# Group norm in pairs of token tiles, a residual shift ahead of the gates, a folded scale, and three rounding passes on GpSimd in a two-layer decoder

## The reference

```python
# gated memory, per token and head: h = values weighted by gates / (maxit + 1e-6)
xn = (h - mean(h)) / sqrt(var(h) + 1e-5)          # over the 32 channels of a head
out = xn * gn_w + gn_b
# quantised feed-forward
def act_quant(x):
    scale = 127.0 / clip(max(abs(x), -1), 1e-5)
    return clip(round(x * scale), -128, 127) / scale
h = act_quant(x) @ weight_quant(w1).T             # 256 -> 1024
h = silu(depthwise_conv(h))
y = act_quant(h) @ weight_quant(w2).T             # 1024 -> 256
```

## Time and profile before

| | |
|---|---|
| median of three runs | 827.95 us |
| the profiled execution | 829.15 us |
| its span, first to last instruction | 827.6 us |
| TensorE busy (matmuls) | 739.1 us, 89% |
| VectorE busy | 574.9 us, 69% |
| ScalarE busy | 358.0 us, 43% |
| GpSimd busy | 170.3 us, 21% |
| filler matmuls | 38 |

### The profile page before, as it was taken

One profiled execution on the slowest core, in us unless ns is written; L12 is line 12 of the kernel. 1 busy time (PEld: TensorE's weight loads), 2 busy tenths in 40 slices (PEclk: granted clock), 3 DMA queues, 4 the chain that ended last, 5 costly groups with the idle time before them and its releaser, 6 DMA issues.

```text
span 827.6 us, 14805 instructions
## 1 busy us (share of the span) xinstructions
PE 739.1 (89%) x5876; PEld 495.7 (60%) x5933; DVE 574.9 (69%) x1477; ACT 358.0 (43%) x654; POOL 170.3 (21%) x257
## 2 busy tenths in 40 slices
PE   9999999989999968799969999999999978975494
PEld 5776565766566755567644576867547757554232
DVE  1568554674476778988899964657465777798786
ACT  2675214242255226476238534243344431683253
POOL 8611001210006120004330030201003631014201
PEclk9999999999999978699989999999999998988597
DMA  9501000000010100013100030000000000000001
GB/s 347 226 14 64 0 1 1 2 2 2 27 51 27 28 1 2 0 52 103 27 0 1 2 102 1 2 1 2 1 1 1 2 2 2 0 2 2 0 1 51
DMA packets 12740, 23.77 MB, mean 29 GB/s; under 512 B 768, under 2 KB 7040, under 8 KB 12416
## 3 DMA queue, kind: packets, MB, share of 16 engines
q1 hardware_dynamic: 12672, 22.82, 8.0%
HBM read 20.72 MB, written 2.10 MB: 28 GB/s over the span
## 4 chain that ended last, share of the span: by engine, by line
PE 70%; DVE 19%; issue 5%; ACT 3%; POOL 2%; DVEq 0%; ACTq 0%; POOLq 0%
PE bank L753 13%; PE bank L571 7%; PE bank L563 7%; PE bank L597 4%; PE bank L851 4%; PE bank L763 3%; PE bank L618 3%; PE bank L1103 3%; PE bank L832 2%; PE bank L739 2%; PE bank L798 2%; PE bank L874 2%; DVE stats L1194 1%; PE bank L556 1%; POOL small L2213 1%
## 5 line engine op out<-in xcount | busy, mean ns | idle before, releaser
L2143 POOL TENSOR_TENSOR rstd<-rstd,minus_half 128x2 f32<-128x2 f32 x56 | 42.6, 761 | 501.1 <-DVE rstd L1200 500.9
L753 PE MATMUL bank<-work,f0w 128*128 128x512 f16 x512 | 114.7, 379 | 0.1
L753 PEld LDWEIGHTS bank<-work,f0w 128*128 128x128 f16 x512 | 49.4, 98 | 59.6 <-issue 1.9
L1926 ACT ACTIVATE work<-bank 128x512 f16<-128x512 f32 x64 | 36.7, 598 | 44.9 <-PE bank L753 33.6
L1410 DVE SCALAR_TENSOR_TENSOR work<-bank,work 128x512 f16<-128x512 f32 x64 | 42.2, 684 | 15.8 <-ACT work L1926 15.5
L1964 ACT ACTIVATE work<-bank 128x512 f32<-128x512 f32 x32 | 19.1, 596 | 73.2 <-PE bank L851 73.1
L618 PE MATMUL bank<-work 128*128 128x256 f32 x208 | 49.9, 382 | 0.0
L851 PE MATMUL bank<-work 64*128 64x128 f32 x512 | 39.0, 294 | 5.0 <-issue 3.2
L2213 POOL TENSOR_TENSOR small<-small,minus_half 128x8 f32<-128x8 f32 x16 | 26.9, 1678 | 69.8 <-DVE small L1647 69.8
L618 PEld LDWEIGHTS bank<-work 128*128 128x128 f32 x208 | 37.6, 190 | 5.3 <-issue 0.5
L1275 DVE TENSOR_REDUCE small<-bank 128x1 f32<-128x512 f32 (+3 forms) x32 | 18.7, 585 | 31.0 <-PE bank L599 20.3
(11 more groups left out here) (310 smaller groups left out, 1727.5 us busy)
## 6 DMA issues: line engine op xcount, KB each, us to landing
work<-in_mask SPq DMA_DIRECT2D x4, 1024.0 KB, 10.3
xT<-in_xT SPq DMA_DIRECT2D x4, 512.0 KB, 4.1
ctxT<-in_ctxT SPq DMA_DIRECT2D x4, 512.0 KB, 6.5
perf_w<-in_k SPq DMA_DIRECT2D x3, 512.0 KB, 12.1
perf_w<-in_perf_w SPq DMA_DIRECT2D x1, 1536.0 KB, 6.1
x<-in_x SPq DMA_DIRECT2D x2, 512.0 KB, 12.3
ctx<-in_w SPq DMA_DIRECT2D x2, 512.0 KB, 12.2
work<-in_w SPq DMA_DIRECT2D x1, 1024.0 KB, 13.7
```

Of the source, the lines that this page charges most:

```text
L753: ins = nc.tensor.matmul(u.bank[:, :], f0w1[:, k, m * P:(m + 1) * P], s.h1[part][:, k, :], start=(k == 0 and part == 0), stop=(k == NF - 1 ...
L1926: nc.scalar.activation(dst[0][:, m, :], u.bank[:, :], ACT.Relu).then_inc(s.high_made.sem, 1)
L2143: nc.gpsimd.tensor_tensor(s.rstd[:, two], s.rstd[:, two], minus_half[:, 0:2], ALU.pow).then_inc(s.rstd_made.sem, 1)
```

## The change

- The group norm works on pairs of tiles. `ratio` stays by tile; the two tiles' results lie in one buffer (`s.pair`, over the weighed keys). The four small operations, the product with gn_w, the square, the reduction, the power, the scale and the residual add are issued once for two tiles. The product is written to y and scaled in place. The order is ratio 0, 1, square, variance of pair 0; the same for pair 1; then scale, stats and normalize of pair 0 and of pair 1. GpSimd has both powers ahead of both rstd.
- GpSimd adds gn_b to the residual ahead of weighing the keys.
- ScalarE's copy of the first scale row multiplies by f1_scale; `hidden` becomes a product of two tensors.
- GpSimd issues finish_q for blocks 1, 3 and 5; the semaphore for rounded blocks becomes two, and the wait of the mask's load covers both.
- TURNS is written anew for all five queues, and KEEP too: 74 entries with 140 fillers for 26 with 38. By stream and round: (0, 0) 5 to 31, (1, 0) 5 to 43, (0, 1) 5 to 31, (1, 1) 23 to 35.

```diff
--- before.py
+++ after.py
@@ -35,46 +35,57 @@
 ROUNDS = B // STREAMS
 TURNS = {
...
 KEEP = {
-    "perf.spread.0 0 0": 1, "mlstm.out2 0 0": 1, "quant.turn1 0 0": 1, "quant.hidden0 0 0": 2, "sign.xT0 0 1": 1,
-    "sign.xT1 0 1": 2, "perf.spread.1 0 1": 1, "quant.turn1 0 1": 1, "sign.xT0 1 0": 1, "perf.fq.1 1 0": 1,
-    "perf.state.1 1 0": 1, "mlstm.out0 1 0": 1, "perf.spread.0 1 1": 1, "perf.fk.1 1 1": 1, "perf.ft.1 1 1": 2,
-    "perf.state.1 1 1": 1, "mlstm.cols 1 1": 1, "mlstm.out0 1 1": 1, "mlstm.out1 1 1": 1, "mlstm.before3 1 1": 1,
-    "quant.turn0 1 1": 3, "quant.turn1 1 1": 1, "quant.hidden0 1 1": 1, "quant.taps0 1 0": 1, "quant.topT 1 1": 7,
-    "quant.row2 1 1": 2
...
+    "quant.row1 0 0": 3, "quant.topT 0 0": 2, "self.score0 0 1": 1, "self.turn0 0 1": 1, "self.turn2 0 1": 1,
+    "self.product1 0 1": 1, "cross.q1 0 1": 1, "cross.product2 0 1": 1, "sign.xT0 0 1": 6, "sign.early 0 1": 6,
...
+    "quant.topT 0 1": 6, "self.score2 1 0": 1, "self.turn3 1 0": 3, "cross.xT0 1 0": 1, "cross.xT1 1 0": 1,
+    "cross.turn0 1 0": 4, "perf.v0 1 0": 1, "perf.qk.0 1 0": 1, "perf.state.0 1 0": 4, "perf.fk.1 1 0": 6,
+    "perf.ft.1 1 0": 4, "perf.state.1 1 0": 2, "perf.score1.1 1 0": 1, "perf.score3.1 1 0": 1, "perf.out0 1 0": 3,
...
+    "quant.row1 1 1": 1, "quant.turn1 1 1": 1, "quant.hidden0 1 1": 1, "quant.taps0 1 0": 1, "quant.topT 1 1": 6,
+    "quant.row2 1 1": 3
 }
@@ -263,6 +274,8 @@
...
     f1_scale = sb("f1_scale", [P, 2])
+    by_gpsimd = (1, 3, 5)
+
     class Stream:
...
@@ -321,15 +334,14 @@
...
         s.l_state = w.cut(NT - 1, NC, LHT, LV1)
-        s.tmps = [w.cut(LH, LV1),
-                  s.kw[:, 0:2, :, :].rearrange("p a h d -> p (a h d)")[:, 0:LH * LV1].rearrange("p (h d) -> p h d", d=LV1)]
+        s.pair = s.kw[:, :, :, :].rearrange("p a h d -> p (a h d)")[:, 0:NT * LH * LV1].rearrange(
+            "p (q t h d) -> p q t h d", q=2, t=2, d=LV1)
         s.part2_row = w.cut(2, T, dt=BF16, parts=LH)
...
         s.edge = s.small[:, 224:248].rearrange("p (t h) -> p t h", h=LH)
-        s.l_den = s.small[:, 128:128 + LH]
-        s.y_groups = s.y[:, :, :].rearrange("p t (h d) -> p (t h) d", d=LD)
+        s.l_den = s.small[:, 104:104 + 2 * LH].rearrange("p (t h) -> p t h", t=2)
         s.den2, s.var = s.small[:, 160:160 + NT * LH], s.small[:, 192:192 + NT * LH]
-        s.sq = [s.rest[:, j, 0:LH * LD].rearrange("p (g d) -> p g d", d=LD) for j in range(2)]
+        s.sq = [s.rest[:, j, :].rearrange("p (t h d) -> p t h d", t=2, d=LD) for j in range(2)]
 
...
@@ -365,12 +377,16 @@
...
         s.decayed = signal("scores_decayed", LH)
-        s.squared, s.group_var, s.group_rstd = (signal(name, NT) for name in ("group_squared", "group_variance", "group_rstd"))
+        s.squared, s.group_var, s.group_rstd = (signal(name, 2) for name in ("group_squared", "group_variance", "group_rstd"))
 
...
         s.compared, s.scaled_hidden = signal("size_compared", NF - 1), signal("hidden_scaled", NF - 1)
-        s.magic_added, s.q2_made = signal("magic_added", NF), signal("hidden_rounded", NF)
+        s.magic_added = signal("magic_added", NF)
+        s.rounded_v = signal("hidden_rounded_by_vector", NF - len(by_gpsimd))
+        s.rounded_g = signal("hidden_rounded_by_gpsimd", len(by_gpsimd))
+        s.q2_made = [(s.rounded_g, by_gpsimd.index(j)) if j in by_gpsimd else (s.rounded_v, j - sum(i < j for i in by_gpsimd))
+                     for j in range(NF)]
         return s
...
@@ -1138,7 +1154,7 @@
...
                 for k in range(NF):
-                    pe.wait_ge(*s.q2_made.at(n, k))
+                    pe.wait_ge(*s.q2_made[k][0].at(n, s.q2_made[k][1]))
                     for t, u in enumerate(several):
...
@@ -1596,15 +1612,12 @@
...
                         ALU.mult).then_inc(u.emptied, 1)
-            weighed = [None] * NT
+            weighed = [None] * 2
 
...
                 yield f"mlstm.ratio{t}"
-                u, tmp = s.banks["mlstm", n, "out", t], s.tmps[t % 2]
-                if t >= 2:
-                    dve.wait_ge(*s.squared.at(n, t - 2))
-                    dve.wait_ge(*weighed[t - 2])
-                if t == 1:
+                u, tmp = s.banks["mlstm", n, "out", t], s.pair[:, t // 2, t % 2, :, :]
+                if t == 0:
                     dve.wait_ge(*s.banks["mlstm", n, "state", NT - 1].full)
...
@@ -1621,56 +1634,62 @@
                     dve.wait_ge(*u.full)
                     dve.wait_ge(*s.banks["mlstm", n, "cols"].read)
                     nc.vector.tensor_copy(tmp, here).then_inc(u.emptied, 1)
-                yield f"mlstm.square{t}"
-                dve.wait_ge(*u.read)
-                at = col["e", t]
-                m = vec.mark(nc.vector.scalar_tensor_tensor(out=s.l_den, in0=tmp[:, :, LD], scalar=-1.0, in1=tmp[:, :, LD],
-                                                            op0=ALU.mult, op1=ALU.max))
+
+            def of_groups(p):
+                return s.y[:, 2 * p:2 * p + 2, :].rearrange("p t (h d) -> p t h d", d=LD)
+
+            def square(p):
+                yield f"mlstm.square{p}"
+                for t in (2 * p, 2 * p + 1):
+                    dve.wait_ge(*s.banks["mlstm", n, "out", t].read)
+                at, g, den = col["e", 2 * p], slice(2 * p * LH, (2 * p + 2) * LH), s.pair[:, p, :, :, LD]
+                m = vec.mark(nc.vector.scalar_tensor_tensor(out=s.l_den, in0=den, scalar=-1.0, in1=den, op0=ALU.mult, op1=ALU.max))
                 dve.wait_ge(*m)
-                m = vec.mark(nc.vector.tensor_tensor(s.l_den, s.l_den, s.cols[:, at:at + LH], ALU.max))
+                m = vec.mark(nc.vector.tensor_tensor(s.l_den, s.l_den, s.cols[:, at:at + 2 * LH].rearrange("p (t h) -> p t h", t=2),
+                                                     ALU.max))
                 dve.wait_ge(*m)
 
                 m = vec.mark(nc.vector.tensor_scalar(s.l_den, s.l_den, 1e-6, 1e18, ALU.add, ALU.min))
                 dve.wait_ge(*m)
-                vec.mark(nc.vector.scalar_tensor_tensor(out=s.den2[:, t * LH:(t + 1) * LH], in0=s.l_den, scalar=EPS, in1=s.l_den, op0=ALU.mult, op1=ALU.mult))
-                weighed[t] = vec.mark(nc.vector.tensor_tensor(
-                    s.rest[:, t % 2, C:2 * C].rearrange("p (h d) -> p h d", d=LD), tmp[:, :, 0:LD],
-                    gn_w.rearrange("p (h d) -> p h d", d=LD), ALU.mult))
-
-            def variance(t):
-                yield f"mlstm.var{t}"
-                g = slice(t * LH, (t + 1) * LH)
-                dve.wait_ge(*s.squared.at(n, t))
-                m = vec.mark(nc.vector.tensor_reduce(s.var[:, g], s.sq[t % 2], AX, ALU.add))
+                vec.mark(nc.vector.scalar_tensor_tensor(out=s.den2[:, g].rearrange("p (t h) -> p t h", t=2), in0=s.l_den, scalar=EPS,
+                                                        in1=s.l_den, op0=ALU.mult, op1=ALU.mult))
+                weighed[p] = vec.mark(nc.vector.tensor_tensor(
+                    of_groups(p), s.pair[:, p, :, :, 0:LD],
+                    gn_w.rearrange("p (h d) -> p h d", d=LD).unsqueeze(1).broadcast_to([P, 2, LH, LD]), ALU.mult))
+
+            def variance(p):
+                yield f"mlstm.var{p}"
+                g = slice(2 * p * LH, (2 * p + 2) * LH)
+                dve.wait_ge(*s.squared.at(n, p))
+                m = vec.mark(nc.vector.tensor_reduce(s.var[:, g].rearrange("p (t h) -> p t h", t=2), s.sq[p], AX, ALU.add))
                 dve.wait_ge(*m)
-                dve.wait_ge(*weighed[t])
+                dve.wait_ge(*weighed[p])
                 nc.vector.scalar_tensor_tensor(out=s.var[:, g], in0=s.var[:, g], scalar=1.0 / LD, in1=s.den2[:, g],
                                                op0=ALU.mult, op1=ALU.add).then_inc(s.group_var.sem, 1)
 
             added = [None] * NT
 
-            def scale(t):
-                yield f"mlstm.scale{t}"
-                dve.wait_ge(*s.group_rstd.at(n, t))
-                dve.wait_ge(*weighed[t])
-                g = slice(t * LH, (t + 1) * LH)
-                m = vec.mark(nc.vector.tensor_tensor(s.y_groups[:, g, :], s.rest[:, t % 2, C:2 * C].rearrange("p (g d) -> p g d", d=LD),
-                                                     s.var[:, g].unsqueeze(2).broadcast_to([P, LH, LD]), ALU.mult))
+            def scale(p):
+                yield f"mlstm.scale{p}"
+                dve.wait_ge(*s.group_rstd.at(n, p))
+                g, two = slice(2 * p * LH, (2 * p + 2) * LH), slice(2 * p, 2 * p + 2)
+                m = vec.mark(nc.vector.tensor_tensor(
+                    of_groups(p), of_groups(p),
+                    s.var[:, g].rearrange("p (t h) -> p t h", t=2).unsqueeze(3).broadcast_to([P, 2, LH, LD]), ALU.mult))
                 dve.wait_ge(*m)
-                dve.wait_ge(*s.shifted.at(n, 2 * NT + t))
-                added[t] = vec.mark(nc.vector.tensor_tensor(s.y[:, t, :], s.y[:, t, :], x_of(s, n)[:, t, :], ALU.add))
-
-            for i in range(NT + 2):
-                if i >= 2:
-                    yield from scale(i - 2)
```

(78 more changed lines are left out.)

13 lines of the change are left out of this document (7 added, 6 removed), and 60 rows, old and new, of tables (KEEP, TURNS).

## The result

The changed kernel takes 837.11 us (median of 4 runs, 835.78 to 839.38), the kernel before 827.81 beside it: ratio 1.0117, 95% interval 1.0104 to 1.0131. It is 9 us slower; 813.0 was forecast, and the range, 801 to 833, does not hold it.

A forecast was written before the change was run, and what follows sets the result against it. VectorE or engine round trips bound the layer tails, TensorE the sign feed-forward. Norm 10.5, passes 3 - 1, gn_b 0.5, folded scale 0.5, clock 9, fillers -7: 15.5 us saved, median 813; range 801 to 833, forecast's own 805 to 819.

The forecast's parts named there:

- What bounds the kernel: Limits differ by stage: TensorE in a stream's sign feed-forward, VectorE or engine round trips in its layer's tail, including the norms.
- The sum: All terms over the whole span: 10.5 + (3 - 1) + 0.5 + 0.5 + 9 - 7 = 15.5 us saved.
- The new order itself I take at 0: Rewritten weave of both streams on all five queues: 0 us, with -6 to +8, as no row shows it.
- Norm by pairs: Four group norms: 10.7 us less VectorE work, 10.5 us of span (2, 2.6, 1.5 and, in the last, 4.4).
- the first pair's power hides behind ratio 2, ratio 3 and the second pair's work: In each norm, GpSimd's first power of 16 columns, about 2.9 us, is covered by some 3.9 us of other work.
- Passes on GpSimd: Rounding of blocks 1, 3, 5: 3 us saved on the path, 1 us lost to contention; 0.8 us a pass.
- gn_b and the folded scale: Additions moved ahead of key weighing, and the hidden pass without its scalar: 0.5 us saved by each.
- Fillers +7, clock -9: TensorE: 102 more filler matmuls cost 7 us, a third of 22; the higher clock gives back 9 us.
- Order, 0 with -6 to +8: New weave of both streams' steps on all five queues, taken as worth nothing within those bounds in us.
- The first: Rival: fillers land on TensorE's path ahead of real matmuls, costing 15 to 22 us; 837 us; slower, chance 0.17.
- The third: Rival: pair's round trips (powers, rstd0) eat the norm's gain, other stream doesn't close up; 825 to 829 us; same, 0.09.
- The fourth: Rival: GpSimd's twelve passes hold VectorE for 8 us by contention; 821 us; chance 0.15, shared with half the gain.

## Why the prediction was wrong, point by point

*What bounds the kernel.* Held. The norm and the roundings lie in VectorE's stretches, and the last norm, from its first ratio to the last scaling, went from 25.1 to 784.18 - 765.48 = 18.7 us, below the 21 forecast, in spite of the wait for the passes (15.7, from 761.96 to 777.66, with all rounding on VectorE).

*The sum.* 15.5 us less was forecast, 9.7 more measured. 13.1 of these 25.2 us are the norm, gn_b, the folded scale and the order together (-11.5 forecast, +1.6 measured: 1.0019), 10.8 the passes on GpSimd (-2 forecast, +8.8 measured), 1.3 the fillers with the clock. So two steps failed: "The new order itself I take at 0", and the passes, taken at 0.8 us each and hidden.

*Norm by pairs, -10.5 us.* The work was sized rightly (8.8 us of VectorE measured alone, 10.7 summed), and so was the power. The step "the first pair's power hides behind ratio 2, ratio 3 and the second pair's work" held in the changed kernel: VectorE waits for no power of the norm there, and for the last norm's two roots 0.58 us and next to nothing once the passes are gone, where 1.3 and 0.8 were put. What failed is that this reaches the end. In the new order the norms seem to give their 11 us, and the lags lose as much outside them. In before's order, which has no such cover, the first and third norms were +3.5 (and +2.6 behind it) and +3.8, the second 0 and the last -2.6 in place of -4.4, and the power's wait is shown to be the cause.

*Passes on GpSimd, -3 and +1.* The largest error that experiments isolate: +8.8. The price was taken from a select on bf16, 0.64 us, and bounded by doubling two-input operations; but GpSimd's time goes by the operations in a pass, and no row behind the two bounds has a subtraction and a minimum over fp32. At 2.0 us against some 1.5 for VectorE to make the next block, it does not keep pace, as the working has it. Nor did the working ask where in GpSimd's own queue a pass stands, and at three of four places that is part of the price. Contention was there, but small. Of VectorE's instructions that ran beside a pass, the products L1786 (677 ns in the mean against 680 without the passes) and L1676 and L1681 of the last norm kept their length; its own rounding passes took 467 against 420 ns, the 4-column product L1794 493 against 222 (three of its four beside a pass), and two normalising passes (L1225) 0.73 us each, a usual one being 0.41. Added up that is 2.6 us in place of the 1 us of the sum. The Trainium skill's rule on shared interfaces (GPSIMD Engine Reference, Key points) names instructions in a 2-port mode and those with two SBUF inputs: the trace doesn't agree with it for the two products of the last norm, both of whose inputs lie in SBUF, though such products did get longer beside GpSimd's two-input weighing, and no run shows the mode of the others. The advice of its section Engine selection, elementwise work on VectorE, held.

*gn_b and the folded scale, -0.5 each.* Nothing alone, within the interval; 3.6 us with the pairs. Which of the two helps them was not tried apart.

*Fillers +7, clock -9.* The net, -2, was near the measured one (-0.7, within the intervals of 0), and both halves were about right: in the lags the fillers cost some 8 us and the clock gave back some 7. The clock rose as forecast (0.964 against 0.97). In 300 to 320 us it went from 1.2 GHz for most of the stretch to 2.4 GHz throughout, which is where 5.4 us come from, and the 16 matmuls of L571 took 3.72 us in place of 6.72. The changed kernel itself is 7.9 us behind before at 298 us and 2.9 at 317. By the Trainium skill (TensorE: Matmul & The Clock Gate, Part 1), activity releases the lower level; the trace agrees, and the fillers that did it cost as much elsewhere.

*Order, 0 with -6 to +8.* Put on top of the pairs as they stand in before's order it is -1.5. Against what the norm was to give in it, it is the 13 us above, more than its upper bound. The cause stays open; the places are 247 to 273 and 705 to 750 us.

*The rivals.* The first gave 837 and was right by accident: in the new order the fillers' cost is balanced by the clock, and only in before's order does their net come to 11 us. The third, savings that do not reach the end, describes the changed kernel without its passes (828.8, in its 825 to 829), though not by the round trips that it names, which that order hides. The fourth gave the right part and, in the main, the wrong mechanism. No rival had the passes' own length and place, which are 8.8 of the 9.7 us.

## What to carry to other kernels

Joining two instructions saves their fixed cost once and lengthens every latency between them; where another stream's steps stand behind the wait on an in-order engine, count them, and join only where the path runs alone or where other work stands between the joined step and its result's first use. Before work goes to an idle engine, price the very form (operations, types, columns) and give its place in that engine's queue: work whose input is ready 9 us before the queue reaches it starts 9 us late, and the longer it is, the later is what is queued behind it. Price fillers against the clock stretch by stretch: here 5.4 us came back in 40 us of the run and were spent in the rest.

## What the hardware showed that I had not expected

GpSimd's time for a one-input pass over 512 columns depends on the operations in it: 0.64 us for a cast from fp32 to bf16, 1.52 with a subtraction, 2.06 with a subtraction and a minimum; VectorE takes 0.42 for the last. Its power grows with the columns, 0.72 us for 2, 1.68 for 8, 2.9 to 3.5 for 16, and a product of the same shapes takes 0.22 to 0.25. Beside GpSimd's passes a VectorE operation over 4 columns took 493 ns in the mean in place of 222, and products of 512 columns kept their 0.68 to 0.69 us. 102 fillers raised the mean granted clock from 0.952 to 0.968 over the whole run and left the time where it was (1.0019 and 1.0011, intervals overlapping).
